# One instruction for both halves of an attention item, and the rotation's swap of halves in GpSimd's addition, in a six-layer local-attention kernel

## What is computed

```
for i in range(6):
    qkv = shift_tokens(x) @ Wqkv[i]                      # 16 heads of 64: q, k, v are 128 x 1024 for an item
    q = l2norm(q) * qs;  k = l2norm(k) * ksc
    q = q * cos * scale + rotate_half(q) * sin * scale   # rotate_half: (x1, x2) -> (-x2, x1)
    k = k * cos / scale + rotate_half(k) * sin / scale
    sim = 8 * q k^T within windows of 32, masked         # each window sees itself and the one before
    x = softmax(sim) v @ Wo[i] + x
    x = ffn(layernorm(shift_tokens(x))) + x              # gated, gelu
```

## Time and profile before

| | |
|---|---|
| median of 3 runs | 1455.85 us (1452.92 to 1457.2) |
| the profiled execution's own time | 1451.59 us |
| its span, first to last instruction | 1449.7 us |
| busy: TensorE, VectorE, ScalarE, GpSimd | 94%, 89%, 87%, 82% |
| mean granted TensorE clock | 0.986 of full speed |
| chain that ended last, by engine | PE 47%, DVE 19%, issue 15%, ACT 6%, POOL 5% |

### The profile page before, as it was taken

How to read it: one execution, slowest core, us unless ns; L and a number is a source line. 1 busy time by engine, 2 the same in 40 slices (tenths; PEclk the granted TensorE clock), 3 DMA queues, 4 the chain that set the end, 5 groups by cost and what they waited for, 6 DMA issues and landing times.

```text
span 1449.7 us, 76627 instructions
## 1 busy us (share of the span) xinstructions
PE 1357.1 (94%) x30176; PEld 1094.5 (75%) x30176; DVE 1294.6 (89%) x2400; ACT 1266.6 (87%) x2523; POOL 1184.0 (82%) x1162
## 2 busy tenths in 40 slices
PE   6589999999999999999999999999999999999985
PEld 4467777877777777777777777777777778777774
DVE  6688999999999999999999999999999999999973
ACT  6578999999999999999999999999999999899873
POOL 2687888888888888888888888888888888888860
PEclk9899999999999999999999999999999999999998
DMA  5221112131111222111122111113111112111111
GB/s 148 81 57 41 38 48 57 36 89 42 51 39 47 57 57 68 42 50 39 47 70 61 50 43 50 39 46 95 36 43 36 36 37 77 43 29 43 43 31 30
DMA packets 61752, 75.09 MB, mean 52 GB/s; under 512 B 8462, under 2 KB 35340, under 8 KB 61708
## 3 DMA queue, kind: packets, MB, share of 16 engines
q1 hardware_dynamic: 61708, 74.51, 18.8%
HBM read 18.90 MB, written 1.05 MB: 14 GB/s over the span
## 4 chain that ended last, share of the span: by engine, by line
PE 47%; DVE 19%; issue 15%; ACT 6%; POOL 5%; DVEq 2%; ACTq 0%; POOLq 0%
PE bank L1275 12%; PE bank L1178 6%; PE bank L1266 6%; DVE ss L906 5%; PE bank L1191 5%; PE bank L1179 4%; PE bank L1180 4%; DVE psum L943 4%; POOL u L444 3%; DVE u L913 3%; PE bank L1228 3%; PE bank L1311 3%; DVE t L922 3%; PE bank L1300 2%; ACT gate L714 2%
## 5 line engine op out<-in xcount | busy, mean ns | idle before, releaser
L444 POOL TENSOR_TENSOR u<-u,t 128x512 f32<-128x512 f32 x384 | 490.5, 1283 | 84.3 <-DVE t L922 68.5
L457 POOL TENSOR_TENSOR u<-u,rn 128x512 f32<-128x512 f32 x384 | 388.9, 1045 | 0.0
L628 ACT ACTIVATE sq<-bank 128x512 f32<-128x512 f32 x384 | 234.0, 610 | 64.0 <-PE bank L1180 62.0
L1178 PE MATMUL bank<-Wl,xsh 128*128 (+1 forms) x576 | 268.0, 465 | 15.4 <-POOL xsl L439 11.3
L463 POOL TENSOR_TENSOR P<-P,rs 128x512 f32<-128x512 f32 x192 | 196.6, 1045 | 95.0 <-DVE rs L948 95.0
L922 DVE TENSOR_TENSOR t<-bank,TS 128x512 f32<-128x512 f32 x384 | 258.7, 684 | 6.1 <-ACT sq L628 2.1
L906 DVE TENSOR_REDUCE ss<-sq 128x8 f32<-128x512 f32 x384 | 255.6, 676 | 6.4 <-issue 6.4
L913 DVE TENSOR_TENSOR u<-bank,TC 128x512 f32<-128x512 f32 x384 | 255.1, 675 | 1.3 <-ACT sq L628 1.3
L652 ACT COPY qkT<-bank 128x512 f32<-128x512 f32 x384 | 225.2, 603 | 13.5 <-PE bank L1191 6.4
L1179 PE MATMUL bank<-Wh,xsl 128*128 (+1 forms) x576 | 228.8, 397 | 0.0
L1180 PE MATMUL bank<-Wh,xsh 128*128 (+1 forms) x576 | 228.7, 397 | 0.0
(11 more groups left out here) (92 smaller groups left out, 2732.1 us busy)
## 6 DMA issues: line engine op xcount, KB each, us to landing
vs<-v SPq DMA_DIRECT2D x384, 128.0 KB, 2.3
Wraw<-in_L_ffn_Wqkv_dram SPq DMA_DIRECT2D x72, 117.5 KB, 2.1
WoS<-in_L_ffn_Wo_dram SPq DMA_DIRECT2D x6, 512.0 KB, 4.0
W1h<-Wh SPq DMA_DIRECT2D x6, 341.0 KB, 2.6
W1l<-Wl SPq DMA_DIRECT2D x6, 341.0 KB, 2.9
Wraw<-in_L_ffn_W_dram SPq DMA_DIRECT2D x12, 116.0 KB, 2.2
out_dram<-X SPq DMA_DIRECT2D x4, 256.0 KB, 2.7
W2S<-in_L_ffn_W_dram SPq DMA_DIRECT2D x6, 128.0 KB
```

Of the source, the lines that this page charges most:

```text
L444: nc.gpsimd.tensor_tensor(u[:, r, c], u[:, r, c], t2[:, r, c % 2], ALU.add).then_inc(add_done[c], 1)
L457: nc.gpsimd.tensor_tensor(by_head(u[:, r, c]), by_head(u[:, r, c]), spread(rn[:, r, HC * c:HC * c + HC], HC, DH), ALU.mult).then_inc(qk_re ...
L1178: nc.tensor.matmul(out, x[0], Wl[:, w], start=True, stop=False)
```

## The change

The eight banks become one tensor `PS` of 8 x 512, and are numbered anew so that many pairs of banks of one item are neighbours (`BANK_USERS` keeps each bank's users and their order, apart from the bank's number). Where they are, one instruction takes both: `v_out`, `exp`, `maxima`, `minus_maxima`, `row_sums` and `divide` for every item, `all_heads_out(0, ...)` for chunks 0 and 1 of both items (k = 2 and 3 stay single), `all_p_out` for r = 0 alone. So in each pair of items VectorE issues 6 instructions fewer, ScalarE 7, GpSimd 2; the others are as wide as before. TensorE's instructions stay; its waits are for the joined instructions' semaphores.

`swapped` no longer exchanges the halves; the sine table is laid out the other way, and `add` on GpSimd reads `t2` with the halves exchanged.

```diff
-        K = [bank(str(k)) for k in range(8)]
+        PS = es.enter_context(nc.psum_tensor("banks", [128, 8, 512], F32))
+        K = [PS[:, k] for k in range(8)]
...
+        HEADS_AT_ONCE, P_AT_ONCE = [[True, True], [False, False]], [True, False]
...
-                 "v": lambda k, r: [v_ready[k]],
-                 "turn_qk": lambda k, r: [qk_out[k]],
-                 "scores": lambda k, r: [sc_out[k]],
-                 "turn_p": lambda k, r: [PT_ready[k]],
+                 "v": lambda k, r: [v_ready],
+                 "turn_qk": lambda k, r: [qk_out[r][k - k % 2 if HEADS_AT_ONCE[k // 2][r] else k]],
+                 "scores": lambda k, r: [sc_out],
+                 "turn_p": lambda k, r: [PT_ready[r][0 if P_AT_ONCE[r] else k]],
...
+        def banks_of(kind, k=0, r=0):
+            b, b2 = (bank_place(kind, k + e, r)[0] for e in range(2))
+            return PS[:, b:b + 2] if b < b2 else PS[:, b2:b + 1][:, ::-1]
...
-                    nc.gpsimd.tensor_tensor(u[:, r, c], u[:, r, c], t2[:, r, c % 2], ALU.add).then_inc(add_done[c], 1)
+                    nc.gpsimd.tensor_tensor(halves(u[:, r, c]), halves(u[:, r, c]), halves(t2[:, r, c % 2])[:, :, ::-1, :],
+                                            ALU.add).then_inc(add_done[c], 1)
...
-                def divide(e, lag, r):
+                def divide(lag, r):
...
+                    nc.gpsimd.tensor_tensor(item(P, r), item(P, r), spread(item(rs, r), 16, DH),
+                                            ALU.mult).then_inc(P_ready, 1)
...
+                def all_heads_out(s, lag, r):
+                    pair = it - lag
+                    act.wait_ge(qk_turned[s], n_(pair * 2 + r) + 1)
+                    act.wait_ge(sc_full[s], n_(pair * 2 + r) - 1)
+                    nc.scalar.copy(qkT[:, r, s].rearrange("p w t (g i) -> p g (w t) i", g=2),
+                                   banks_of("turn_qk", 2 * s, r).rearrange("p g (k i) -> p g k i", i=64)
+                                   ).then_inc(qk_out[r][2 * s], 1)
...
-                    nc.scalar.copy(v[:, r, 512 * j:512 * j + 512], bank_of("v", j, r)[:]).then_inc(v_ready[j], 1)
+                    nc.scalar.copy(v[:, r].rearrange("p (j n) -> p j n", j=2), banks_of("v", 0, r)).then_inc(v_ready, 1)
...
                 if on(1):
-                    heads_out(0, 1, 0)
+                    all_heads_out(0, 1, 0)
                     square(1, 1, 1)
-                    heads_out(1, 1, 0)
                     heads_out(2, 1, 0)
...
                     heads_out(3, 1, 1)
-                    heads_out(1, 1, 1)
+                    all_heads_out(0, 1, 1)
                 if on(2):
                     inverse_deviation(2)
-                if on(1):
-                    heads_out(0, 1, 1)
...
-                    nc.vector.tensor_tensor(halves(t2[:, r, c % 2]), halves(bank_of("chunk", c, r)[:])[:, :, ::-1, :],
-                                            TS[:, layer(it - lag), c % 2].broadcast_to([128, HC, DH]).rearrange(
-                                                "p h (a d) -> p h a d", a=2), ALU.mult).then_inc(t2_done[c], 1)
+                    nc.vector.tensor_tensor(by_head(t2[:, r, c % 2]), by_head(bank_of("chunk", c, r)),
+                                            TS[:, layer(it - lag), c % 2].broadcast_to([128, HC, DH]),
+                                            ALU.mult).then_inc(t2_done[c], 1)
...
                 if on(1):
-                    row_sums(0, 1, 0)
                 if on(0):
                     squares(1, 0, 0)
                 if on(1):
-                    row_sums(1, 1, 0)
+                    row_sums(1, 0)
                     reciprocals(1, 0)
```

More of the change, by code:

```diff
@@ L261, in bank_left, with when_left, both_left, item @@
                 other, ok, orr, lag = users[at]
[L262 to L267 removed]
+                away = users[place][3] + turns - lag
+                if not isinstance(pair, int) or 0 <= pair + away < PAIRS:
+                    return [(s, other in COUNTS_PAIRS, orr, away) for s in FREED[other](ok, orr)]
+            return []
+        def when_left(pair, users):
+            for s, per_pair, r, away in users:
+                if per_pair:
+                    yield s, n_(pair + away + (LAYER_PAIRS if s is h_ready else 0)) + 1
+                else:
+                    yield s, n_((pair + away) * 2 + r) + 1
+        def bank_left(pair, kind, k=0, r=0):
+            return when_left(pair, user_before(pair, kind, k, r))
+        def both_left(pair, kind, k, r):
+            first, second = user_before(pair, kind, k, r), user_before(pair, kind, k + 1, r)
+            return when_left(pair, first + [user for user in second if user not in first])
         def column(at, pair, per=1, k=0, rows=slice(0, 128)):
             return fc[rows, ds(pair // LAYER_PAIRS * per + (at + k), 1)]
+        def item(t, r):
+            if len(t.shape) == 5:
+                return t[:, r].rearrange("p e g c -> p (e g) c")
+            return t[:, r].rearrange("p e g -> p (e g)")
         def layer(pair):
@@ L674, in o_out, with all_p_out @@
+                def all_p_out(lag, r):
+                    pair = it - lag
+                    act.wait_ge(P_turned, n_(pair * 2 + r) + 1)
+                    act.wait_ge(pv_full, n_(pair * 2 + r) - 1)
+                    nc.scalar.copy(PT[:, r].rearrange("p e (t g i) -> p g (e t) i", g=2, i=64),
+                                   banks_of("turn_p", 0, r).rearrange("p g (k i) -> p g k i", i=64)
+                                   ).then_inc(PT_ready[r][0], 1)
                 def o_out(h, lag, r):
@@ L754, in step @@
                     masks(0, 1, 1)
-                    v_out(1, 1, 1)
-                    exp(1, 1, 0)
-                    exp(0, 1, 0)
+                    exp(1, 0)
                 if on(0):
@@ L1039, in step @@
                 if on(1):
[L1040 to L1043 removed]
+                    maxima(1, 1)
+                    minus_maxima(1, 1)
                 if on(2):
```

184 lines of the change are left out of this document (82 added, 102 removed).

## The result

| | us, median (lowest to highest) | ratio to before, 95% interval |
|---|---|---|
| before | 1454.38 (1448.48 to 1457.2), 4 runs | |
| changed | 1487.62 (1485.72 to 1489.88), 4 runs | 1.0235 [1.0197, 1.0272] |

Slower by 33 us. The forecast was 1499 in a range of 1456 to 1516: right in sign, over a third too large in size (45.5 us for 33).

What follows compares the result with a forecast made beforehand. The prediction took one closed loop through four engines, 28.14 us a turn, as the bound. Its terms 0.24 + 0.44 + 0.31 gave 0.99 us a turn, 45.5 us over 46 turns: forecast 1499 us, range 1456 to 1516.

Steps and rivals of the forecast that it cites:

- B: Start of a turn: joined `all_heads_out(0, 1, 0)` on ScalarE ends later, so TensorE's `turn_qk(1, 1, 0)` starts later, +0.44 us a turn.
- C: Middle of the turn: joined `all_heads_out(0, 1, 1)` on ScalarE delays `lvx`, `rstdx` and VectorE's `normal`, +0.31 us a turn.
- rival 1: Occupancy decides: VectorE's work sets the turn, six joins save 0.48 us a turn, faster, 1434 us; chance 0.14.
- TensorE's idle time ahead of batch 2: Sign: TensorE's wait before its second batch of q/k turns, `turn_qk(1, 1, 0)`, grows from 0.22 to about 0.66 us.
- Place A: Just before `turn_qk(1, 1, 0)`: joined `v_out` of item 0 on ScalarE delays TensorE's `turn_qk(0, 1, 0)`, +0.24 us a turn.
- the subtraction: Joined `minus_maxima` of item 1 on VectorE delays `v_chunk(1, 0, 0)` by 0.21 us, counted 0 beside the +0.24 of `v_out`.
- Nothing that is joined stands between `turn_p` and `project_out`: Claim behind the +0.44 us of `all_heads_out(0, 1, 0)`: nothing of that delay is given back on this way.
- The zeros: Parts priced at 0 us a turn: remaining joins, hidden by waits or unneeded first halves, and the exchange of halves.
- the exchange: Moved from VectorE's product to GpSimd's addition: 0.01 us saved at most on VectorE, +0.12 to -0.24 on GpSimd, taken as 0.
- Rival 2: One place only: just the joined `all_heads_out(0, 1, 0)` counts, 20 us, 1476 us; chance 0.24.
- Rival 3: The exchange costs GpSimd +0.12 us an addition, one in the loop, 5.5 us more than the sum, 1505 us; chance 0.08.
- Rivals 1 and 4: The fourth rival: nothing comes of it, gains and delays cancel, 1456 us; chance 0.04. For the first see rival 1.

Runs made afterwards that it cites:

- e1: Changed kernel with the joined copy of turned q/k of token group 0 (`all_heads_out(0, 1, 0)`) in two copies again; 1466.89 us, ratio 1.0081.
- e2: Changed kernel with the joined copy of turned q/k of token group 1 in two, one behind the inverse deviation; 1471.76 us, ratio 1.0109.
- e7: Changed kernel with `v_out` of item 0 and `minus_maxima` of item 1 in two instructions each again; 1481.52 us, ratio 1.02.
- e8: e3 with the copy of turned q/k of token group 0 (`all_heads_out(0, 1, 0)`) joined again; 1467.1 us, ratio 1.0086.
- e3: Changed kernel with four joins undone: turned q/k of both token groups, `v_out` of item 0, `minus_maxima` of item 1; 1451.26 us, ratio 0.9974.
- e4: Changed kernel with the exchange of halves back in VectorE's product and GpSimd's addition straight, all joins kept; 1487.44 us, ratio 1.0211.
- e12: Kernel before with one join alone, the two exponentials of a token group in one instruction; 1462.91 us, ratio 1.0063.

## Why the prediction was right, and where not

**The kind of bound: right.** "One closed loop through four engines", where "what lengthens an element of it lengthens every turn; what is saved on an engine beside it is saved into a wait": ScalarE's 22 us less of work came back as nothing, and undoing a join made the kernel faster at B and at C. The Trainium skill (Perfetto Trace Analysis, Optimizing Scalar/DVE Operations) says that breaking up instructions may pay where ScalarE and VectorE aren't saturated but cause bubbles on others. e1 and e2 agree, with 20.7 and 15.9 us for a second instruction each. It says as well that grouping can help if the engine is saturated, which is rival 1. That is not borne out for the change as a whole, at 89% and 87% busy.

Of the signs that the prediction listed, `lvx` came 0.47 us behind the variance (0.45 said), the turn was 28.9 us (29.1), TensorE's idle time ahead of batch 2 0.51 (0.66), VectorE's share 87% (85%), the joined copy 1.03 us (1.05 to 1.07).

**Place C, +0.31: right**, 0.35 at `up` and 0.34 in the turn (changed less e2), with a second way beside it that I had not seen and that TensorE's idle 0.37 us ahead of `up` covers.

**Place A and the subtraction, +0.24, side by side: right at the place** (0.25 between e7 and changed, 0.24 between e8 and e2), **wrong at the turn's end**, where 0.13 arrive. The term that is missing is a gain: with `v` joined TensorE takes 0.24 us from the copy to batch 2, not the 0.34 that I carried over from the earlier trace rows.

**Place B, +0.44: right for the second half, too large for the turn.** Beside e3 the second half costs 0.44 at batch 2 (e8). Of that 0.08 falls into a wait of `turn_p` for the divide, which the joined exponential had made late, and 0.04 more is gone by the end of the turn: 0.32 arrive. "Nothing that is joined stands between `turn_p` and `project_out`" looked behind the delay; what took part of it is a second wait that ends at `turn_p` itself. The agreement of 0.44 with 0.44 is in part luck: against the kernel before, which the prediction meant, batch 2 is later by 0.34 in e8, since its single copy took 0.63 us and started later.

**The zeros**: the exchange, right on both engines (e4). The other joins: right in sum, -0.06 us a turn (before less e3), but not one by one, since the exponential's zero needs joins beside it, and by the rows those of the row sums and the divide (e12).

The sum by what the runs show: from e3's 28.12, B gives 0.32 (e8 less e3), `v` and `minus` 0.13 (e2 less e8), C 0.34 (changed less e2), which is 28.91; e3 itself is 0.06 under the kernel before; together 0.73 for the 0.99 predicted. Of the 0.26 too many, 0.12 are B's, 0.11 those of A, 0.06 the small gain, and C was 0.03 too few.

**Rival 2**, one place alone, 1476: refuted by e1 and e2, though the time lies midway between it and the forecast. **Rival 3** by e4. **Rivals 1 and 4** fall with the result, a loss clear of noise. What stays open is why the join of `v` changes the order of TensorE's waits, why the copy at place B is shorter with the exponential joined, and where the last 0.04 us of B's delay goes.

**e3 beats both kernels, the one before by little**: 0.9974 [0.996, 0.9989], and again 0.9981 [0.9963, 0.9999]. It joins where a whole chain is joined (exponential, row sum, divide) or where the prediction found nobody in the loop waiting for a first half.

## What to carry to other kernels

Before joining two instructions, ask for each half who waits for it. If another engine takes the first half, the join delays it by the whole second half, 0.44 us here on ScalarE, and saves its own engine 0.05 to 0.09 us (0.15 for GpSimd's divide); in a loop closed over several engines the delay is paid every turn. Joins along a chain belong together: the same join was worth a little beside the other joins, its followers among them, and cost 0.6% alone. That the followers' joins make the difference is read from the rows; no run joins just these three. And price a delay where it ends, at the next turn's start, not where it begins: of 0.44 and 0.25 us at their places, 0.32 and 0.13 arrived. Look there also for a second wait that ends at the same instruction: such waits made `v` and `minus` free beside each other, and took part of B's delay.

## What the runs showed of the hardware

GpSimd's addition of 512 elements takes 1286 ns when it reads `t2` with the two 32-element halves of each head exchanged (changed), and 1282 to 1283 when it reads it straight (e4, before). VectorE's product from PSUM takes 683 ns without the exchange (changed), and 683 to 684 with it (e4, before). What I had not expected most is how much one wait in TensorE's queue weighs when it stands behind the one that ends last: with three entries behind the copy's end batch 2 starts 0.34 to 0.35 us after it, with two 0.24, in all fourteen traces.
